# Where a coming tile's transposes stand in the last five steps: ahead of the slot's attention and routing work, or behind it

## What is computed

```
x = x + attn0(layernorm(x))
x = x + ffn0(layernorm(x))
x = x + attn1(layernorm(x))
z      = layernorm(x)
scores = z @ Wg.T                         # per token, 8 experts
w      = softmax of the two best scores
y      = sum over the two experts e of  w[e] * (silu(z @ W1[e].T) * (z @ W2[e].T)) @ W3[e].T
x = x + y
```

## Time and profile before

| what | value |
| --- | --- |
| runs of the kernel, device us | 1270.61, 1276.05, 1283.96 (median 1276.05) |
| profiled execution, device us | 1274.81 |
| its span | 1273.1 us |
| mean granted TensorE clock | 0.926 of full |
| tile 0's slot begins (up, L619) | 948.5 us |
| tile 34's slot begins | 1080.2 us |

### The profile page before, as it was taken

The page is one execution under the profiler, slowest core; times in us unless marked ns, Lnnn a source line. Parts: engine busy times, 40 slices in busy tenths (PEclk is TensorE's granted clock), DMA queues, the critical chain, the costliest instruction groups (busy, mean ns, idle before and its releaser), DMA issues.

```text
span 1273.1 us, 27497 instructions
## 1 busy us (share of the span) xinstructions
PE 1088.8 (86%) x8482; PEld 897.5 (70%) x8482; DVE 738.2 (58%) x1989; ACT 573.6 (45%) x1254; POOL 441.5 (35%) x602
## 2 busy tenths in 40 slices
PE   2989999999989799999999999998758989697770
PEld 2656667667656688888888888887647767576650
DVE  3566676766753365556666666665665556445533
ACT  2155554554544334455555555554444444343330
POOL 4244344444422111123334343434531113224516
PEclk9799999999998699999999999999859999798885
DMA  6444444444440271101111111112332223234535
GB/s 215 126 143 117 122 135 117 128 126 121 124 118 25 91 253 33 32 26 42 43 41 41 41 41 41 41 63 71 92 91 70 81 76 124 100 117 138 146 127 162
DMA packets 98292, 122.17 MB, mean 96 GB/s; under 512 B 16022, under 2 KB 85852, under 8 KB 98204
## 3 DMA queue, kind: packets, MB, share of 16 engines
q1 hardware_dynamic: 91292, 102.17, 26.5%
q0 software_dynamic: 6912, 18.88, 4.7%
HBM read 64.37 MB, written 56.10 MB: 95 GB/s over the span
## 4 chain that ended last, share of the span: by engine, by line
PE 58%; DVE 15%; ACT 9%; issue 9%; POOL 3%; another core or an unknown queue 2%; DMA 2%; DVEq 1%; SPq 1%; ACTq 0%; POOLq 0%
PE bank L927 4%; PE bank L840 3%; PE bank L1550 3%; PE bank L1552 3%; PE bank L1551 3%; DVE a_negm L1255 3%; PE bank L842 3%; PE bank L841 3%; PE bank L604 2%; PE bank L619 2%; PE bank L959 2%; PE bank L631 2%; PE bank L621 2%; PE bank L620 2%
## 5 line engine op out<-in xcount | busy, mean ns | idle before, releaser
L1136 ACT ACTIVATE a_prob<-bank 128x512 f32<-128x512 f32 x192 | 114.3, 598 | 137.9 <-PE bank L927 137.4
L1550 PE MATMUL bank<-b_xF_hi,wff_hi 128*128 128x256 f32 x512 | 153.7, 300 | 2.4 <-DVE b_xF_lo L1922 1.4
L1255 DVE TENSOR_REDUCE a_negm<-bank 128x2 f32<-128x512 f32 (+1 forms) x192 | 129.9, 685 | 33.0 <-PE bank L894 32.8
L1551 PE MATMUL bank<-b_xF_lo,wff_hi 128*128 128x256 f32 x512 | 145.5, 284 | 0.4 <-issue 0.4
L1552 PE MATMUL bank<-b_xF_hi,wff_lo 128*128 128x256 f32 x512 | 145.4, 284 | 0.0
L1360 POOL TENSOR_SCALAR_AFFINE_SELECT a_prob<-a_prob 128x1024 f32<-128x1024 f32 x64 | 70.0, 1094 | 172.0 <-ACT a_prob L1136 172.0
L927 PE MATMUL bank<-a_Q,a_K 50*128 50x256 f32 (+1 forms) x512 | 108.4, 314 | 1.5 <-DMA a_Q<-bias_rows 1.1
L894 PE MATMUL bank<-a_K,a_Q 48*128 48x256 f32 (+1 forms) x512 | 108.5, 313 | 0.0
L1930 DVE TENSOR_TENSOR b_hf<-bank,b_sg 128x256 f32<-128x256 f32 x128 | 53.9, 421 | 92.9 <-ACT b_sg L1775 90.8
L1550 PEld LDWEIGHTS bank<-b_xF_hi,wff_hi 128*128 128x128 f32 x512 | 97.9, 191 | 7.5 <-DVE b_xF_lo L1922 1.8
L784 POOL DMA_INDIRECT m_ring<-y_sorted,b_k_rows x64 | 61.5, 961 | 114.3 <-DMA y_sorted<-m_y 75.8
(11 more groups left out here) (270 smaller groups left out, 3190.5 us busy)
## 6 DMA issues: line engine op xcount, KB each, us to landing
scr<-a_split SPq DMA_DIRECT2D x64, 256.0 KB, 2.4
a_Q<-scr SPq DMA_DIRECT2D x192, 64.0 KB, 2.2
a_K<-scr SPq DMA_DIRECT2D x192, 64.0 KB, 2.3
m_xs<-x_sorted SPq DMA_DIRECT2D x78, 128.0 KB
y_sorted<-m_y SPq DMA_DIRECT2D x78, 128.0 KB
x_sorted<-b_r_zeros SPq DMA_DIRECT2D x1, 6016.0 KB, 20.0
parts<-b_split SPq DMA_DIRECT2D x16, 256.0 KB
out<-x_res SPq DMA_DIRECT2D x16, 256.0 KB
```

The costliest lines, as they stand in the source:

```text
L1136: nc.scalar.activation(o, src, ACT.Exp, scale=float(HD) ** -0.5).then_inc(S.exps, 1)
L1255: nc.vector.tensor_reduce(R.negm[:, p, j, c0:c0 + n], ps[bank][:, :].rearrange("p (h k) -> p h k", h=n), axis=AX.X, op=ALU.max, negate=Tru ...
L1550: pe.matmul(o, wh, xh, start=(c == 0), stop=False)
L1551: pe.matmul(o, wh, xl, start=False, stop=False)
```

## The change

The two transposes and two copies of a coming tile (`xT`) become functions of their own, `pe_next`, `act_next` and `dve_next`. The steps call the tile's work with `next_too=False` and call these functions behind the slot's pieces. The slots after the steps (tiles 35 on) keep the old order, as the default is `next_too=True`. No instruction is added or dropped, waits and their counts stay, and the exponentials of slot 3 stay behind everything, now also behind a later `act_next`.

```
-            def pe(eng, i):
-                def xT(k):
+            def pe_next(eng, i):
+                k = i + 2
+                if k < NTILES:
                     eng.wait_ge(S.loaded[k % 4], 16 * (k // 4 + 1))
                     if k >= 1:
                         eng.wait_ge(S.xT_lo, k)
...
+            def pe(eng, i, next_too=True):
...
                 if i >= 2:
                     down(i - 2)
-                if i + 2 < NTILES:
-                    xT(i + 2)
+                if next_too:
+                    pe_next(eng, i)
...
@@ pe_step
                     if with_tile(t, m):
-                        X1["pe"](pe, tile_of(t, m))
+                        X1["pe"](pe, tile_of(t, m), next_too=False)
...
                     if m == 2 and live(t):
                         pe_down(pe, t, 0)
+                    if with_tile(t, m):
+                        X1["pe_next"](pe, tile_of(t, m))
@@ act_step
-                        X1["act"](act, tile_of(t, m))
+                        X1["act"](act, tile_of(t, m), next_too=False)
...
                     if live(t):
                         act_h(act, t, m)
+                    if with_tile(t, m):
+                        X1["act_next"](act, tile_of(t, m))
                     if m == 3 and live(t - 3):
                         for u in range(U):
                             act_exp(act, t - 3, u)
@@ v_step
-                        X1["dve"](dve, tile_of(t, m))
+                        X1["dve"](dve, tile_of(t, m), next_too=False)
...
                         prepare_layer1(dve, (m - 2) // 2)
+                    if with_tile(t, m):
+                        X1["dve_next"](dve, tile_of(t, m))
                     if isinstance(t, int) and (t, m) in LO_AT:
                         v_weights(dve, LO_AT[t, m])
```

More of the change, by code:

```diff
@@ L654, in pe @@
                     offsets(0)
-                    xT(0)
-                    xT(1)
+                    pe_next(eng, -2)
+                    pe_next(eng, -1)
                     eng.wait_ge(wf.lo1, NMAIN)
@@ L669, in pe, with act_next @@
                     down(i - 2)
[L670 to L675, removed]
+                if next_too:
+                    pe_next(eng, i)
+            def act_next(eng, i):
+                k = i + 2
+                if k < NTILES:
                     eng.wait_ge(S.xT_ps, k + 1)
@@ L679, in xT, with act @@
                     nc.scalar.copy(R.xT_hi[:, k % 2, :], ps[XT][:, 0:E]).then_inc(S.xT_hi, 1)
+            def act(eng, i, next_too=True):
                 def silu(k):
@@ L699, in act @@
                 if i == 0:
-                    xT(0)
-                    xT(1)
+                    act_next(eng, -2)
+                    act_next(eng, -1)
                 if i < NTILES:
@@ L707, in act @@
                     y(i - 2)
-                if i + 2 < NTILES:
-                    xT(i + 2)
+                if next_too:
+                    act_next(eng, i)
             done = [0]
@@ L724, in add, with dve_next @@
                                                op0=ALU.mult, op1=ALU.add).then_inc(S.added, 1)
-            def dve(eng, i):
-                def xT(k):
+            def dve_next(eng, i):
+                k = i + 2
+                if k < NTILES:
                     eng.wait_ge(S.xT_hi, k + 1)
@@ L731, in xT, with dve @@
                                             ALU.subtract).then_inc(S.xT_lo, 1)
+            def dve(eng, i, next_too=True):
                 def h(k):
@@ L751, in dve @@
                         nc.vector.memset(R.h[:, k, :], 0.0).then_inc(S.count, 1)
-                    xT(0)
-                    xT(1)
+                    dve_next(eng, -2)
+                    dve_next(eng, -1)
                 if i < NTILES:
@@ L757, in dve @@
                     hT(i - 1)
-                if i + 2 < NTILES:
-                    xT(i + 2)
+                if next_too:
+                    dve_next(eng, i)
                 if i == TOKENS[1].tile:
@@ L788, in pool @@
                     first = end_item[g]
-            return dict(sp=sp, pe=pe, act=act, dve=dve, pool=pool, table=v_table, sums=sums)
+            return dict(sp=sp, pe=pe, act=act, dve=dve, pool=pool, table=v_table, sums=sums, pe_next=pe_next,
+                        act_next=act_next, dve_next=dve_next)
         def attention(region):
```

## The result

The kernel after took 1289.96 us (median, 1281.82 to 1297.79); the kernel before, run again beside it, 1279.95. The ratio is 1.0077, 95% interval 1.004 to 1.0114: about 9.9 us slower, inside the range and within 1%, but twice the +4.9 us forecast. The profiled execution took 1289.98 with a span of 1288.3, 15.2 over the one before. That is more than the medians differ by: tile 0 already begins 3.2 us later in it (951.75 against 948.54), where the changed code has not run yet.

A forecast was written before the change was run, and what follows sets the result against it. TensorE, busy 86% of the span, was taken as the bound, with tile-chain delays lost one for one. The terms summed to +4.9 us, giving 1279.7 for the profiled execution and a median of 1281 us, range 1268 to 1291.

The forecast's parts named there:

- The exchange of waits: On the tile chain: moved transposes stop waiting for hT's low part, but hT may wait for xT's; +4.9 us in all.
- Slot 0, +2.1: Tiles 3, 11, 19: hT waits behind VectorE's rank and last piece, slot 1's wait goes; net +0.7 us, three times.
- Slot 7, +1.3: Tiles 2, 10, 18: hT comes 0.8 us later, about 0.3 comes back; +0.5 twice and +0.3 for tile 18.
- that term, held at 0: Tile 1: a wait of 1.01 us goes, but hT comes later behind `v_rope` and the low part; gain 0.
- Slot 3, +1.65: Tiles 6, 14: table load for the exponentials begins 1.37 us later behind `pe_main`; +1.35 for tile 14, +0.3 for tile 6.
- Covered waits, -1.05: Tiles 9, 13, 17 and 21: pieces cover waits and give 0.3, 0.3, 0.25 and 0.2 us; -1.05 us.
- Sum of the waits: Whole kernel: 2.1 + 1.3 + 1.65 - 1.05 + 0.7 + 0.2 = +4.9 us.
- Rival 2: TensorE's clock falls more often at eight new waits, 1.13 us each; +13.9 us, 1290 us, chance 0.13.
- more than six stretches: Sign that the forecast is wrong: over six stretches at the lower clock between tiles 0 and 34.
- The tile 35 mark: Sign that the forecast is right: tile 35 comes 3 to 7 us later against tile 0.
- Rival 1: VectorE and ScalarE run far enough ahead, readiness decides and the pieces hide waits; -6.1 us, 1270 us, chance 0.13.
- Rival 3: Standstill beside GpSimd's fills near 1090 us shifts: 1274.6 if gone, 1287.4 if once more; chance 0.12, half each side.

The follow-up runs named there:

- e_only0: The kernel before with the change made in slot 0 alone (tiles 3, 11, 19, 27), on all three engines; ratio 1.0032 to the kernel before.
- e_not0: The changed kernel with slot 0 put back in the old order; ratio 1.0062 to the kernel before.
- e_not3: The changed kernel with slot 3 put back in the old order; ratio 1.0059 to the kernel before.
- e_light: The kernel before with the change made in slots 1, 2, 4, 5 and 6 alone; ratio 1.0000 to the kernel before.
- c_after: The changed kernel run again as a control, no edit; 1287.4 us, ratio 1.0075 to the kernel before.
- e_fill_busy: The changed kernel with the six `up` matmuls issued twice in tiles 5, 6, 13, 14, 21 and 22; ratio 1.0079 to the kernel before.
- the new bank: hT in a bank apart from xT from tile 11 on: kernel before 1271.68 us, 0.9936; changed kernel 1279.46 us, 1.0024.

## Why the prediction came out as it did

**The exchange of waits: right; as the main cause of the loss: wrong.** hT waits for the low part of the moved piece, 5.3 us in eight waits; of the waits of L605 for L755 none is left in slots 1, 2 and 6. e_only0 and e_not0 switch the waits on and off by slot. But the forecast let these waits make the whole loss, and most of it is TensorE's busy time at the lower clock. The median came out 9 us over the forecast's 1281 and still inside the range: 3.9 of these are the base, which came out at 1279.95 and not 1276.05, and 5.0 the change.

**Slot 0, +2.1: right in kind, displaced.** Its waits were 1.26 to 1.28 where TensorE ran at the full clock (forecast 1.3 to 1.6). I had put the mark at tiles 3, 11 and 19, but this hT stands one slot later, at tiles 4, 12 and 20, and in the kernel after only tile 20 shows it, for at the other two `up` was slowed by as much. e_only0 puts the slot at 0.32%, 4.0 us, with an interval that holds the 2.1.

**Slot 7, +1.3: a little low.** hT waited 0.99, 1.00 and 0.65 (forecast 0.8, 0.8 and, with what comes back taken off, 0.3): +2.6 before what comes back. There is also a wait of 0.81 in tile 2's slot, behind slot 6's rope, in exchange for the 1.01 that went in tile 1's: that term, held at 0, was nearly right.

**Slot 3, +1.65: a little low.** The table load came 1.7 later (forecast 1.37), tile 15's slot is 1.7 us longer (1.35), tile 7's 0.8 (6.4 against 5.6): 2.5 against 1.65. e_not3 against the change puts it at 0.18%, 2.3 us, within the uncertainty.

**Covered waits, -1.05: the gain did not come.** e_light is at 1.0000. Its low clock is 6 us up over all executions, with an uncertainty of 7; at 0.32 that would be 1.8 us, enough to have eaten the gain. Not separated.

**Sum of the waits: too high, or hidden.** Up to tile 33 TensorE's idle time rose by 2.2 us in one profile and 1.5 in the other, against a sum of 4.9. The 4.5 and 2.4 up to tile 34 hold a part of the standstill. Some waits forecast, at tiles 4 and 12, were covered by matmuls at the lower clock, so idle time alone can't tell what the exchange would have cost at the full one.

**The mis-sized term: the clock, priced at nothing in the forecast and held apart as Rival 2.** It measured 9.7 and 7.1 us of busy time in the two profiles, and stood 29 us longer at the lower clock in the mean of c_after's executions. I had it all or nothing, eight separate stretches of 1.13 each, with "more than six stretches" as the mark. What came was mainly longer ones: six of up to 10.2 us, where before had four of 3.4. Counted literally, the mark was missed; by time, 29.9 us more at the lower clock are nearly nine stretches of 3.4, about the +9.0 of that rival. What spoke against it in the prediction, one wait of 0.85 that left the next slot's clock at 1.00, was one case, in a stretch with fewer waits around it. So the forecast should have held a term for the clock; its size could not be read from the rows of before. Rival 2's +13.9 is nearly as far from the measured +9.9 as the forecast's +4.9 is, on the other side, and that its 1290 is the measured median to the microsecond is luck, for it was counted from a base 3.9 lower. The Trainium skill, TensorE: Matmul & The Clock Gate, "A second HAM failure mode: psum-queue depth-cycling", gave the right warning, of a clock that swings where TensorE often idles briefly between groups of matmuls. The trace agrees that the clock swings more (0.85 against 0.95), but not on which idles do it: e_fill_busy recovered the clock without filling the waits of hT, and slot 0's waits moved it in the mean of e_only0's executions by no more than the uncertainty. The tile 35 mark (3 to 7 us later against tile 0) came out at 12.8 and 9.2 for this reason.

**Rival 1** fell: the low part follows the queue's order (1008.43, 1008.88). **Rival 3** is not needed: the standstill of ScalarE and TensorE near tiles 33 to 35 is there in both, 16.5 us before and 17.6 after for these slots. What starts it was not tried.

**Open:** what decides the amount of low clock in one execution, and why the change raises it; and why the new bank brings 6 to 8 us when its waits were worth 2 to 3. That single profiles do not rank the variants as the medians do is not open: e_only0's stretch, 142.2 us, is longer than e_not0's, 138.9, because the profiled execution of e_only0 took 1257.03 us at a clock of 0.924, where the median of its runs in the ratio is 1246.56 and their mean clock 0.935.

## What to carry to other kernels

A piece that is moved to cover one wait takes its own successors with it: find what waits for its copies, and which pieces now stand ahead of them in each engine's queue. And when TensorE is the bound, write the loss as idle time plus clock: here an exchange of gaps that looked even, 1 us against 1 us, went with longer stretches at half clock, and each us of these cost about 0.32 us. One profile is not enough to see it; compare the mean clock of all executions. Where two transposes share a bank only for want of space, look first whether another is free by then.

## What was not expected of the hardware

Added matmuls came at no measured cost. 36 of them (about 5.8 us at the full clock) left the kernel at 1.0038 and 1.0079, by where they stood, against 1.0075 without them; the time at the lower clock in the profiled stretch was 20.6 and 19.4 us, against 36.0. Within one kernel the low clock scattered by 7.5 us between two executions. And between the chips the kernel before differed by 3%, 1278 us on the first against 1242 on the other two. Tile 34's slot took 11.5 to 13.6 us in the profiles of the first and 4.3 to 5.2 on the other two, and the kernel before stood 190 us at the lower clock on the first and 155 on each of the others.
